# Layer input turned by transposing transfers instead of TensorE in the attention half of a conditioned transformer layer

## The reference

```python
cond = silu(c) @ wc.T + bc
sh1, sc1, g1, sh2, sc2, g2 = jnp.split(cond, 6, axis=-1)
h = _ln(x) * (1.0 + sc1) + sh1
x = x + g1 * _gqa_attn(h, wq, wk, wv, wo)      # 16 query heads, 4 key heads, head size 32
h = _ln(x) * (1.0 + sc2) + sh2
x = x + g2 * _mlp(h, w1, b1, w2, b2)           # 512 -> 2048 -> 512, exact gelu
```

## Time and profile before

| what | us |
|---|---|
| time, median of 3 runs | 1416.37 (1415.76 to 1417.13) |
| the profiled execution | 1415.25 |
| its span in the trace | 1413.2 |
| busy TensorE products | 1381.5 |
| busy TensorE weight loads | 994.0 |
| busy VectorE | 867.5 |
| busy ScalarE | 748.4 |
| busy GpSimd | 640.0 |

### The profile page before, as it was taken

The page is one execution under the profiler, slowest core; times in us unless marked ns, Lnnn a source line. Parts: engine busy times, 40 slices in busy tenths (PEclk is TensorE's granted clock), DMA queues, the critical chain, the costliest instruction groups (busy, mean ns, idle before and its releaser), DMA issues.

```text
span 1413.2 us, 19177 instructions
## 1 busy us (share of the span) xinstructions
PE 1381.5 (98%) x6733; PEld 994.0 (70%) x6733; DVE 867.5 (61%) x1455; ACT 748.4 (53%) x1349; POOL 640.0 (45%) x279
## 2 busy tenths in 40 slices
PE   6999999999999999999999999999999999999998
PEld 4655665666656566565568888788888888888886
DVE  3778787677778767687653364755475355733243
ACT  6376758576675757666743456524443344422321
POOL 3067687686867768587810175412031010311012
PEclk9999999999999999999999999999999999999999
DMA  8332322423232232323257665477662865446423
GB/s 289 90 88 57 81 80 82 122 82 102 57 96 92 83 122 78 109 57 95 70 161 238 152 199 147 161 253 194 183 194 73 302 187 159 154 157 195 148 81 120
DMA packets 149295, 190.44 MB, mean 135 GB/s; under 512 B 45817, under 2 KB 70409, under 8 KB 149201
## 3 DMA queue, kind: packets, MB, share of 16 engines
q1 hardware_dynamic: 149200, 189.23, 44.3%
HBM read 108.91 MB, written 40.93 MB: 106 GB/s over the span
## 4 chain that ended last, share of the span: by engine, by line
PE 83%; DVE 6%; ACT 3%; SPq 3%; DMA 2%; POOL 2%; issue 1%; DVEq 0%; ACTq 0%; POOLq 0%
PE acc L2330 17%; PE proj_bank L1180 13%; PE turn L2317 9%; PE key_bank L1264 8%; PE pv_bank L1273 8%; PE row_bank L1251 7%; PE up L2317 6%; PE acc L2281 4%; PE up L1599 4%; DVE neg_max L994 2%; PE sum_bank L1283 2%; SPq L559 2%; SPq L1647 1%; DMA gate_now<-gate_scratch 1%; PE turn L1583 1%
## 5 line engine op out<-in xcount | busy, mean ns | idle before, releaser
L994 DVE TENSOR_REDUCE neg_max<-row_bank 128x1 f32<-128x512 f32 x512 | 337.7, 684 | 139.8 <-PE row_bank L1251 135.6
L818 ACT ACTIVATE probs<-key_bank 128x512 f32<-128x512 f32 x512 | 299.6, 598 | 159.4 <-PE key_bank L1264 157.4
L689 POOL TENSOR_TENSOR probs_sum<-probs_sum,probs 128x2048 f32<-128x2048 f32 x62 | 285.5, 4605 | 14.2 <-ACT probs L818 7.3
L2330 PE MATMUL acc<-w_t,hidden 128*128 128x512 f32 x1152 | 269.3, 390 | 0.3 <-DVE hidden L2175 0.3
L2330 PEld LDWEIGHTS acc<-w_t,hidden 128*128 128x128 f32 x1152 | 215.8, 188 | 46.6 <-DVE hidden L2175 1.6
L1264 PE MATMUL key_bank<-q_stack,k_stack 128*128 128x512 f32 x512 | 217.5, 428 | 3.2 <-ACT probs L818 2.8
L1251 PE MATMUL row_bank<-k_stack,q_stack 96*128 96x512 f32 x512 | 203.3, 408 | 4.0 <-DVE neg_max L994 2.4
L689 POOL TENSOR_TENSOR probs_sum<-probs 128x2048 f32<-128x2048 f32 x31 | 142.6, 4600 | 82.0 <-ACT probs L818 82.0
L1785 POOL TENSOR_TENSOR y<-y,resid 128x512 f32<-128x512 f32 x30 | 41.0, 1398 | 269.2 <-DVE y L2096 269.2
L1264 PEld LDWEIGHTS key_bank<-q_stack,k_stack 128*128 128x128 f32 x512 | 96.1, 188 | 83.2 <-issue 46.9
L1251 PEld LDWEIGHTS row_bank<-k_stack,q_stack 96*128 96x128 f32 x512 | 96.3, 188 | 38.4 <-DVE neg_max L994 16.7
(11 more groups left out here) (214 smaller groups left out, 1862.1 us busy)
## 6 DMA issues: line engine op xcount, KB each, us to landing
ring<-w1s_scratch SPq DMA_DIRECT2D x168, 256.0 KB, 3.5
q_stack<-spare SPq DMA_DIRECT2D x384, 64.0 KB, 2.0
hid_scratch<-spare SPq DMA_DIRECT2D x36, 256.0 KB, 3.8
spare<-hid_scratch SPq DMA_DIRECT2D x36, 256.0 KB, 2.6
xa<-in_x_dram SPq DMA_DIRECT2D x8, 1024.0 KB, 9.6
resid<-in_x_dram SPq DMA_DIRECT2D x8, 1024.0 KB, 7.1
x_scratch<-resid SPq DMA_DIRECT2D x8, 1024.0 KB, 4.5
spare<-in_L_cond_w_dram SPq DMA_DIRECT2D x32, 256.0 KB, 3.4
```

Source lines behind the costliest of these rows:

```text
L689: nc.gpsimd.tensor_tensor(probs_sum[:, :, :], first_in[:, :, :], probs[kt][:, :, :], ALU.add).then_inc(added, 1)
L818: nc.scalar.activation(probs[kt][:, r, :], key_bank[r % 2][:, :], ACT.Exp).then_inc(exp_done, 1)
L994: nc.vector.tensor_reduce(out=neg_max[:, g % 2, i:i + 1], in_=row_bank[(g + i) % 2][:, :], op=ALU.max, axis=AX.X, negate=True).then_inc(ro ...
L2330: last = nc.tensor.matmul(acc[tt][:, :], hidden[n % 2][i][:, tt * P:tt * P + P], w_t[:, j, 2 + k, :], start=(own == 0 and m == 0), stop=(o ...
```

## The change

The T tokens no longer make TensorE work, except for sequences 0 and 1. In sequence b the x of sequence b + 2, once normalised, is copied by ScalarE as half-words into two planes per tile (`halve`, 8 activations), turned by 8 transposing transfers which SyncE issues in two portions (`turn_tiles`), and copied back into `xa` by ScalarE (`join`, 8 activations). In the next sequence a T token is only the modulation and the high part on ScalarE and the low part on VectorE, from `xa`. That holds for the attention inputs of sequences 2 to 7 and the MLP input of sequence 0.

To make room in memory the queries of a group stand in one of three places (`q_ring`), no longer four, `v_full` shares its place with `gated[1]`, and small buffers of the front lie in the new ones. All three fill tables and the beats of the statistics, the normalisation and the softmax sums are set anew. GpSimd makes 1/std after the adds of group 1 instead of group 2.

The diff, cut to what the text speaks of:

```diff
 FILL = {
-    (0, 0): ("Q3a", "Q3b", "Q3c", "Q3d T0"),
-    (0, 1): ("", "", "VT", ""),
-    (0, 2): ("T1", "T2", "", ""),
+    (0, 0): ("Q3ab", "T0", "Q3c T1", "Q3d"),
+    (0, 1): ("T2 VT", "", "", ""),
+    (0, 2): ("T3", "Ka", "Kb", ""),
...
-    (2, 3): ("", "Q1b", "Q1c", "Q1d"),
-    (3, 0): ("", "Q2a", "Q2b", "Q2c"),
+    (2, 3): ("Q2a", "", "Q1b", "Q1c"),
+    (3, 0): ("Q1d", "", "Q2b", "Q2c"),
...
+Q_RING = HKV - 1
+PE_TURNED = 2
 SUM_AT = (1, 1)
-LN_AT = (2, 0)
+LN_AT = (1, 3)
 INVERT_AT = (2, 1)
-REFINE_AT = (2, 2)
+REFINE_AT = (2, 1)
...
-STATS_AT = (40, 41, 43, 44)
-MOMENTS_AT = 51
-EPS_AT = 51
-SHIFT_AT = 54
-NORM_AT = (54, 55, 59, 63)
+STATS_AT = (23, 28, 29, 30)
+MOMENTS_AT = 32
+EPS_AT = 34
+SHIFT_AT = 35
+NORM_AT = (35, 36, 37, 40)
+HALVE_AT = (38, 41, 42, 46)
+JOIN_AT = (58, 59, 62, 63)
...
-        v_full = sb(st, "v_full", [P, N])
+        v_full = gated[1]
...
-        q_stack = sb(st, "q_stack", [P, HKV, R, N], f32r)
+        q_ring = sb(st, "q_ring", [P, Q_RING, R, N], f32r)
...
+        halves = sb(st, "halves", [P, TT, 2, D], u16)
+        planes = sb(st, "planes", [P, 2, KD, N], u16)
+        x_halves = xa[:, :, :].bitcast(u16).rearrange("p t (d i) -> p t i d", i=2)
...
+        def turned_no(b):
+            return b - PE_TURNED
+        def lowered(b, kt):
+            return turned_no(b) * KD + (kt + 1)
+        def queries(b, g):
+            return q_ring[:, group_no(b, g) % Q_RING, :, :]
...
+            def turn_tiles(b, tiles):
+                for tt in tiles:
+                    if tt == 0 and b > PE_TURNED:
+                        sp.wait_ge(joined, turned_no(b) * 2 * KD)
+                    sp.wait_ge(halved, turned_no(b) * 2 * TT + 2 * tt + 2)
+                    for i in range(2):
+                        sp.dma_start_transpose(planes[:, i, :, tt * P:tt * P + P], halves[:, tt, i, :]).then_inc(turned, 16)
...
                 if has_next:
-                    sp.wait_ge(proj_ready, u.ready("T3"))
+                    if has_last:
+                        sp.wait_ge(h_lowered, lowered(b + 1, KD - 1))
+                    else:
+                        sp.wait_ge(proj_ready, u.ready("T3"))
...
                     stack_k(1)
-                    stack_q(u, 0)
+                    stack_q(u, b + 1, 0)
+                    turn_tiles(b + 2, (0, 1))
                 stack_max(b, 3)
                 if has_next:
                     sp.wait_ge(keys_scored, exps_no(b, 3, 0))
                     stack_k(2)
-                    stack_q(u, 1)
+                    stack_q(u, b + 1, 1)
+                    turn_tiles(b + 2, (2, 3))
                     stack_max(b + 1, 0)
...
                     for kt in range(1, TT):
                         add_probs(b, g, kt)
-                    if g == HKV - 2:
+                    if g == 1:
                         rstd_of(b + 2)
...
+            def halve(b, tt):
+                if tt == 0 and b > PE_TURNED:
+                    act.wait_ge(turned, turned_no(b) * 128)
+                act.wait_ge(normed, b * TT + (tt + 1))
+                for i in range(2):
+                    nc.scalar.activation(halves[:, tt, i, :], x_halves[:, tt, i, :], ACT.Copy).then_inc(halved, 1)
+            def join(b, kt):
+                act.wait_ge(halved, turned_no(b) * 2 * TT + 2 * TT)
+                act.wait_ge(turned, turned_no(b) * 128 + 128)
+                for i in range(2):
+                    nc.scalar.activation(x_halves[:, kt, i, :], planes[:, i, kt, :], ACT.Copy).then_inc(joined, 1)
+            def modulate_next(b, kt, scale, shift):
+                if kt == 0:
+                    act.wait_ge(cond_copied, b + 1)
+                act.wait_ge(joined, turned_no(b) * 2 * KD + 2 * kt + 2)
+                nc.scalar.activation(xa[:, kt, :], xa[:, kt, :], ACT.Identity,
...
+            def h_high_next(b, u, kt):
+                act.wait_ge(modulated, b * KD + (kt + 1))
+                act.wait_ge(proj_ready, u.ready("Q3"))
+                nc.scalar.activation(h[0][:, kt, :], xa[:, kt, :], ACT.Copy).then_inc(h_hi, 1)
...
+                if n in HALVE_AT and has_next:
+                    halve(b + 2, HALVE_AT.index(n))
+                if n in JOIN_AT and has_next:
+                    join(b + 2, JOIN_AT.index(n))
                 for name in ended(n - COPY_LAG, has_last, has_next):
-                    if name[0] == "T":
+                    if name[0] == "T" and has_last:
+                        h_high_next(b + 1, u, int(name[1]))
+                    elif name[0] == "T":
                         h_high(b + 1, u, int(name[1]))
...
+            def h_low_next(b, kt):
+                dve.wait_ge(h_hi, b * KD + (kt + 1))
+                nc.vector.tensor_tensor(h[1][:, kt, :], xa[:, kt, :], as_f32(h[0][:, kt, :]), ALU.subtract).then_inc(h_lowered, 1)
...
                 if 0 in tiles:
                     room(u, "K")
-                pe.wait_ge(proj_taken["dve"], u.taken(f"T{max(tiles)}"))
+                if b < PE_TURNED:
+                    pe.wait_ge(proj_taken["dve"], u.taken(f"T{max(tiles)}"))
+                else:
+                    pe.wait_ge(h_lowered, lowered(b, max(tiles)))
...
-                elif name[0] == "T":
-                    turn_x(b + 1, int(name[1]), u)
+                elif name[0] == "T" and b + 1 < PE_TURNED:
+                    turn_x(b + 1, int(name[1]), u)
+                elif name[0] == "T":
+                    return
```

137 lines of the change are left out of this document (75 added, 62 removed).

## The result

The changed kernel takes 1493.73 us (median of 5 runs, 1489.64 to 1496.08) against 1416.37 before: ratio 1.0544, 95% interval 1.0530 to 1.0558, 77.4 us more. Its profiled execution took 1489.64 us with a span of 1487.6, 74.4 more than the span before.

A forecast was written before the change was run, and what follows sets the result against it. TensorE's own work, busy 98% of the span, was taken as the bound. The terms gave -1.8 + 6.1 + 4.6 + 0.7 = +9.6 us in sequences 1 to 6, +60.3 over all sequences, so 1477 us; range 1442 to 1505.

The forecast's parts named there:

- Two holds: TensorE held at beat 27 by late x, 6.1 us, and from score 61 by late planes, 4.6 us a sequence.
- Term 1: T tokens of sequences 1 to 7 lose 112 transposes on TensorE: 1.8 us less per sequence, 12.3 in all.
- what I had put at nothing: No cost from three query places, shared v_full, front or MLP; maxima behind transposing transfers 0, at worst 0.5 us.
- Term 2: VectorE's statistic in beat 23 waits over 8 us for x, holding TensorE before beat 27: 6.1 us per sequence.
- My own sign of being wrong: Wrong if VectorE's statistic finds x landed, or if TensorE has other work while it waits.
- What was to take its place if x came sooner: 1/std behind GpSimd's adds, ending some 52 us after T0, asked for in beat 35 near T0 + 45: about 6 us.
- Term 3: ScalarE's first join in beat 58 waits 3.5 us for the turned planes; joins included, 4.6 us per sequence.
- the heavier rival: Both holds, with transposing transfers at 1.76 us and the low clock after both in full: +85.7, 1502 us; chance 0.14.
- Term 4: TensorE's clock drops to its lower level after the hold before beat 27: 0.7 us per sequence, between 0 and 1.3.

The follow-up runs named there:

- all_early: The changed kernel with x, gate row and residual issued before beat 16's scores, and the last transposing transfers behind group 3's row maxima: 1416.18 us, 0.9997.
- join_narrow: all_early with each join copy on ScalarE cut to 16 of 512 columns: 1407.24 us, 0.9931 of the kernel before.
- join_vector: all_early with the eight join copies of a sequence on VectorE instead of ScalarE, in the same beats: 1478.36 us, 1.0433 of the kernel before.
- gate_first: The changed kernel with gate row and residual issued before the wait for beat 16's scores, x left behind the queries: 1470.39 us, 1.0375 of the kernel before.

## Why the prediction was right, and where it was wrong

The forecast was 1477, measured 1493.7, inside the range, and the sign is the one forecast. Two holds, in the two places named, are all of the loss: without them the kernel takes what it took before.

**Term 1: its reason failed, its size stays open.** The failed step is "This is on the path, since TensorE is the bound". In the kernel before it was not: with three quarters of those transposes left out, nothing changes (1.0006), where my working gives 9.2 us. A busy share of 98% was the whole argument. But TensorE's busy rows stretch where it is paced by VectorE's row maxima and ScalarE's exponentials two steps behind (84 products less took 1.7 us off its busy time), and a piece taken out of such a stretch comes back at the next such wait. In the new order something was won all the same, in the stretch where the transposes had stood. I had put beat 27, with no hold, at T0 + 34.5; all_early has it at 35.4 on average, of which 1.3 are the joins' backlog of beats 0 to 2, and join_narrow at 34.1. Whether the transposes or the moved parts won this, no run tells.

Of the 16.7 us by which the forecast was low, about 12 are not in the holds: without them the forecast is -12.3, and measured is nothing (0.9997). They are term 1 and what I had put at nothing, together.

**Term 2 had the size by luck and the wrong cause.** The failed step is "The gate row makes VectorE wait two beats earlier too, but for less than x, so it adds nothing". The gate row is what holds: it lands at T0 + 34.1, VectorE has asked for it since 27.4, and x alone out of the way gives nothing (1.0543 against 1.0544), gate row and residual give 23 us, in which x lands sooner too, and all three 38.6. My own sign of being wrong was there: while the statistic waits for x, for 3.0 us and not 7 to 9, TensorE has other work (busy without a pause from 468 to 472). With the gate row out of the way x costs 15.3 us (1470.4 - 1455.1), 2.5 a sequence, where I had put 6.1. I had worked out beat 27 from x's landing at T0 + 38.8 (measured 39.9), and put 40.6; measured 40.9 to 42.4. The waits for gate row and x are in series on one engine, and the second lay under the lower clock behind the first. Terms 2 and 4 together were 6.8 us a sequence in the forecast (40.8 for six), and 38.6 in all measured. What was to take its place if x came sooner, GpSimd's chain near T0 + 52, did not come: with gate row, residual and x sooner, ScalarE has 1/std at T0 + 49 after a wait of 1.4 us. The residual was sooner too, on which that chain stands.

**Term 3 was right**, place and cause: ScalarE's first copy waits 4.83 us (forecast 3.5) for the planes, which are late because of the queries in SyncE's queue. Forecast 4.6 a sequence and 4 in sequence 0, 31.6; measured 36.9. Two things that I had not counted go with the 5 us more: two join copies take 1.39 us, not 1.1, and the low clock came here too, which I had given to the heavier rival.

**Term 4** was right in kind: in the 4 us behind each hold the granted clock is 0.50 to 0.61. How much of the 38.6 and the 36.9 is the clock's was not measured by itself. Beats 61 to 64 take 3.7 to 4.0 us with the hold of term 3 and 2.3 to 2.55 without it.

**What I had put at nothing** holds in sum only. The failed step is "The copies themselves [...] lie in ScalarE's 27 us of air where they are spread": the joins' own time costs 9 us (join_narrow) when nothing waits for the planes, 1.3 us a sequence of it before beat 2 of the next. Term 3 had counted 1.1 of it, on top of its wait of 3.5. TensorE's waits for the maxima add 3, and the slow low part in sequence 7 some 0.8. What the halving copies cost was not tried. About as much must have been won, since all_early comes out level, and without the joins' time the kernel is 9.9 us below the one before (0.9931): sequences 1 to 6 are 2.7 us shorter each, more than the 1.8 of term 1. Beats 2 to 27 are where it was won. What won it stays open: the transposes alone, in the old order, win nothing; the new tables with and without the transposes were not compared.

## What to carry to other kernels

Before a transfer is blamed, list every wait that its engine meets ahead of it: of two in series only the first may count, and taking away the second alone shows nothing. A busy share near 100% on an engine that is fed two steps ahead does not say that each piece of its work is on the path; leave a piece of it out and look at the next wait. On a queue that issues in order, put transfers that are asked for soon ahead of long groups of small ones: here that alone was worth 77 us.

## What the runs showed of the hardware

A copy of 128 x 512 half-words on VectorE, alone, takes 0.45 us (median of 56 in join_vector, 0.43 at least), and up to 4.78 when GpSimd is in an add over 128 x 2048 words; it ends 0.3 us after the add. A subtraction with both inputs in SBUF is stretched too, up to 4.69 instead of 0.68 (all_early). VectorE's row maxima, statistics and gatings at 0.68 us are not stretched by the same adds. The Trainium skill (GPSIMD Engine Reference, Key points) states a contention between the two engines for some of VectorE's instructions, those in a 2-port mode or with two inputs in SBUF. The trace agrees for the subtraction, which has two. The half-word copy has one; by that rule it would be in a 2-port mode, which no run here shows, but it too waits for the whole of GpSimd's instruction.

ScalarE's half-word copies, in pairs: 1.16 us for two from the words into halves, 1.40 for two back from planes into words. One instruction over both planes takes 1.38, and one over both halves 1.06: the time goes with the elements far more than with the instructions.

In the attention of the changed kernel TensorE is held 15 times for more than 1.5 us. Its clock fell to its lower level behind all seven holds of 4.0 us and more and behind five of the eight shorter ones (2.4 to 3.5 us), not behind the other three (2.3, 2.8 and 3.1). Behind the hold of 4.35 us in beat 23 it stayed there for some 6 us, and products of 512 columns took 0.63 us instead of 0.40.

The transposing transfers kept the price of the earlier trace rows: 1.27 us to issue and 2.5 to land (median of 56), also while queries were under way. A gate row of 256 KB took 4.6 us to land with residual and x behind it; x, 1 MB, took 9.4 behind the residual and 6.4 without it (gate_first).
